# One reordering in three places: the opening of a strided attention and the fronts of two expert stages

## The chip, the cores and the metric

The kernel runs on one core of one Trainium2 chip. The metric is the device time of one execution in microseconds (us). Engines: TensorE (PE; PEld is its weight load), VectorE (DVE), ScalarE (ACT), GpSimd (POOL) and SyncE (SP), which only issues transfers. They run side by side, each in the order of its own program, and wait for one another by semaphores.

## The reference, cut to what matters

Four layers in a row, each with a tanh gate and a residual, over x of 8 batches x 100 tokens x 512:

```python
x = x + tanh(g_xattn[0]) * perceiver_attention(ctx, layernorm(x), mask)
x = x + tanh(g_ffn[0]) * experts_top2_of_4(layernorm(x))      # stage f
x = x + tanh(g_xattn[1]) * strided_attention(layernorm(x), ctx)   # stage g
x = x + tanh(g_ffn[1]) * experts_top2_of_8(layernorm(x))      # stage m
```

The strided attention has 16 heads of 32; head h attends to every 16th context row from row h on, 45 keys per batch and head:

```python
Q = x @ Wq.T + bq;  K = ctx @ Wk.T + bk;  V = ctx @ Wv.T + bv
scores = Q_h @ K_h[h::16].T / sqrt(32)
attn = softmax(scores)
out = concat_h(attn @ V_h[h::16]) @ Wo.T + bo
```

An expert stage takes layernormed tokens, chooses two experts per token by their logits, weighs them with a softmax over the two, and sums `silu(x @ W1) * (x @ W3) @ W2` of both.

## The kernel before, in words

Products in f32 that need more than one pass are made of three products of a high and a low part: ScalarE makes the high part by a copy to the fp32r type, VectorE or GpSimd the low part by subtraction ("split").

**Stage g, `strided_attention`.** TensorE first makes keys and values of four groups of heads (`context(c)`) and the queries of two halves of the batches (`half(h)`) in banks 0 to 3 of PSUM, in turn; ScalarE copies them out (`move_keys`, `move_values`, `move_queries`). The last are `context(3)`, whose keys sit in bank 2 and values in bank 3. Meanwhile ScalarE makes the high parts of the output weights (`high_output_weights`), two of four among the last queries and two after `move_values(3)`, and after them waits for the gate and makes its tanh; VectorE makes the low parts (L2701) and scales the output bias by the gate (L2703, `bo_done`), whereupon GpSimd adds the bias to the residual of 8 batches (L2311).

Then comes the work by batch n. TensorE: `scores(n)` (L2504) in banks 0, 1 or 2, 3 by the parity of n; `element(b)` (L2496), the transposes that turn the values of batch b, in banks 4 to 7, copied by ScalarE (L2393) to `v_nat`; `transposes(n, r)` (L2512) of the probabilities in banks 4 and 5, copied by ScalarE and, as r runs from 0 to 3, `attend(n)` (L2521) in bank 6; `project(n)` (L1265 to L1267 with `g_wo_hi`, `g_wo_lo`) in bank 7. VectorE: `lower(n)`, the row maxima (L2658) and their subtraction (L2661); ScalarE: `exponent(n)` (L2397); VectorE: `divide(n)`, row sums (L2667), reciprocal and multiply (L2669); then `low_output(n)` (L2680), `finish(n)` (L2674).

Before the change TensorE's order at the opening is: wait for all four banks, `scores(0)`, eight elements, `scores(1)`, wait for all element copies, then for n = 0 to 7 `transposes(n, 0..1)`, `scores(n + 2)`, `transposes(n, 2..3)`, `project(n - 1)`, `attend(n)`. VectorE's is low weights, bias, `lower(0)`, `divide(0)`, `lower(1)`, `divide(1)`. ScalarE's is four elements, `exponent(0)`, four elements, `exponent(1)`, then the loop.

**Stages f and m, `gated_experts`.** Both run the same code. Tokens are sorted into slots of 128 by expert, 14 in f and 16 in m. VectorE computes, from rank tables made before, the place of each token in a slot: `picked` (L1880), `filled` (L1884), a chain of some ten linked operations, four comparisons `at_row` (L1909); TensorE sums 16 matmuls (L1752) into the row numbers; VectorE casts them to `rows_at` (L1922), and GpSimd gathers each slot's rows from DRAM by an indirect transfer into `y_acc[:, s]` (L1631). Before the gathers the same `y_acc[:, s]` holds piece s of the raw weights, so gather s waits for the low split of piece s:

```python
if q == 0 and s < DIRECT:
    wait_low(pool, 0, 0, s)
```

The 16 pieces of the first group are split high by ScalarE (L1676) and low by VectorE (L1916). VectorE's order is: maximum and subtraction of the logits (L1876, L1877), `picked`, rank copy (L1881), the chain, three splits, `rows_at` (L1922, L1924, L1925), the fourth split, the gates (L1969 to L1975, eight operations), a wait for the first gather to land, splits 4 to 15 with two tiles of low tokens among them. ScalarE's is four splits, Exp and Tanh and a Silu to load its table, 12 splits, the tokens' high parts (L1686). TensorE transposes slots 0 and 1 (L1765) and goes through the slots (L1780 to L1784), ScalarE and VectorE making silu and product (L1699, L1952).

## Time and profile before

| | us |
|---|---|
| median of 3 runs | 2011.34 |
| lowest and highest | 2009.47 and 2014.04 |
| profiled execution, its time | 2012.05 |
| profiled execution, its span | 2010.3 |
| mean granted TensorE clock | 0.972 of full speed |
| stage f, from its first instruction | from 990.7 |
| stage g, from its first matmul | from 1513.1 |
| stage m, from its first instruction | from 1648.4 |

The span runs from the first to the last instruction of the profiled execution; all times of rows are counted from its start. The clock is the share of 2.4 GHz that the throttle granted. "Busy" leaves out waits and the issuing of transfers.

### The profile page before, as it was taken

The page shows a single profiled execution, that of the slowest core. Times are in us where ns is not written, and L with a number is a line of the kernel's source. Part 1 is how long each engine was busy: PE and PEld are TensorE (multiplying, and loading weights), DVE is VectorE, ACT ScalarE, POOL GpSimd, SP SyncE. Part 2 cuts the span into 40 slices and gives each one's busy share as a digit, 9 for nine tenths or more (in the row PEclk, how much of TensorE's full clock was granted, in tenths as well). Part 3 has the DMA queues.
Part 4 walks back from the last instruction along what each step waited for, and adds up shares of the span by engine and source line. Part 5 has one row for each costly group of instructions (what it writes and reads, how often), then busy time and mean ns, then how long its engine had stood idle before and what let it go on. Part 6 is the DMA issues. An engine that isn't in the chain of part 4 may idle for free. (4 is left out here: it accounts for less than half of the span.)

```text
span 2010.3 us, 35337 instructions
## 1 busy us (share of the span) xinstructions
PE 1888.3 (94%) x12144; PEld 1538.6 (77%) x12144; DVE 1051.9 (52%) x2437; ACT 801.9 (40%) x1733; POOL 648.9 (32%) x529
## 2 busy tenths in 40 slices
PE   7999999999999999999599999999997877999994
PEld 4788787887878787878378888888884766999983
DVE  6526565655656565646553333233345675644564
ACT  4434343433434343433433334233323544555550
POOL 4030202002030302000145553455521215787872
PEclk9999999999999999999799999999998987999997
DMA  7741013121221210010343333133368044635546
GB/s 290 239 137 53 25 41 81 41 81 40 55 66 55 66 47 35 9 27 14 108 120 111 111 115 125 43 114 110 115 231 306 12 160 121 209 138 179 192 153 210
DMA packets 122363, 220.26 MB, mean 110 GB/s; under 512 B 41883, under 2 KB 46779, under 8 KB 120295
## 3 DMA queue, kind: packets, MB, share of 16 engines
q1 hardware_dynamic: 117415, 202.62, 30.3%
q0 software_dynamic: 4800, 15.73, 2.4%
q8 instruction: 85, 1.39, 0.3%
q14 instruction: 63, 0.52, 0.1%
HBM read 189.47 MB, written 28.03 MB: 108 GB/s over the span
## 5 line engine op out<-in xcount | busy, mean ns | idle before, releaser
L588 POOL TENSOR_TENSOR a_cols<-a_cols,a_moments_b 128x722 f32<-128x722 f32 x32 | 58.4, 1825 | 546.0 <-DMA a_moments_b<-a_moments_dram 518.0
L757 PE MATMUL a_kv_ps<-a_kvin_hi,a_wk_hi 128*128 128x512 f32 (+1 forms) x512 | 196.0, 383 | 0.0
L758 PE MATMUL a_kv_ps<-a_kvin_lo,a_wk_hi 128*128 128x512 f32 (+1 forms) x512 | 179.9, 351 | 0.0
L759 PE MATMUL a_kv_ps<-a_kvin_hi,a_wk_lo 128*128 128x512 f32 (+1 forms) x512 | 179.8, 351 | 0.0
L1952 DVE TENSOR_TENSOR f_h_sb<-f_h_sb,f_banks 128x256 f32<-128x256 f32 x112 | 47.2, 421 | 242.3 <-ACT f_h_sb L1699 241.8
L669 ACT ACTIVATE a_probs<-a_probs,a_neg_max 100x822 f32<-100x822 f32 x128 | 125.9, 984 | 101.3 <-DVE a_neg_max L1056 101.3
L1265 PE MATMUL f_banks<-f_wab_hi,f_x_hi 128*128 x392 | 161.2, 411 | 0.0
L1699 ACT ACTIVATE f_h_sb<-f_banks 128x256 f32<-128x256 f32 x112 | 43.0, 384 | 291.9 <-PE f_banks L1267 263.9
L757 PE MATMUL a_kv_ps<-a_wv_hi,a_kvin_hi 128*128 128x512 f32 (+1 forms) x384 | 156.7, 408 | 0.3 <-DVE a_k_lo L1049 0.3
L1267 PE MATMUL f_banks<-f_wab_hi,f_x_lo 128*128 x392 | 154.2, 393 | 0.0
L1266 PE MATMUL f_banks<-f_wab_lo,f_x_hi 128*128 x392 | 153.0, 390 | 0.0
L759 PE MATMUL a_kv_ps<-a_wv_hi,a_kvin_lo 128*128 128x512 f32 (+1 forms) x384 | 152.2, 396 | 0.0
L758 PE MATMUL a_kv_ps<-a_wv_lo,a_kvin_hi 128*128 128x512 f32 (+1 forms) x384 | 151.4, 394 | 0.0
L659 ACT ACTIVATE a_probs_t<-a_t_ps 128x400 f32<-128x400 f32 x128 | 64.3, 502 | 187.4 <-PE a_t_ps L843 187.4
L652 ACT ACTIVATE a_k_hi<-a_kv_ps 128x512 fp32r<-128x512 f32 (+1 forms) x128 | 65.8, 514 | 175.8 <-PE a_kv_ps L759 167.2
L1265 PE MATMUL m_banks<-m_wab_hi,m_x_hi 128*128 x448 | 133.7, 298 | 0.0
L1623 POOL TENSOR_TENSOR f_wy_lo<-f_raw,f_wy_hi 128x512 fp32r<-128x512 f32 x60 | 77.3, 1288 | 160.1 <-ACT f_wy_hi L1676 160.1
L1056 DVE CUSTOM_DVE_ANT_0 a_probs<-a_s_ps,a_mask_add 100x822 f32<-100x822 f32 x128 | 128.5, 1004 | 0.0
L1267 PE MATMUL m_banks<-m_wab_hi,m_x_lo 128*128 x448 | 126.7, 283 | 0.0
L1266 PE MATMUL m_banks<-m_wab_lo,m_x_hi 128*128 x448 | 126.3, 282 | 0.0
L1069 DVE COPY a_probs_t<-a_t_ps 128x300 f32<-128x300 f32 x128 | 59.8, 467 | 124.3 <-PE a_t_ps L843 124.0
L843 PE MATMUL a_t_ps<-a_ident,a_probs 100*128 100x100 f32 x896 | 122.6, 253 | 0.7 <-DVE a_probs_t L1069 0.7
(440 smaller groups left out, 4901.8 us busy)
## 6 DMA issues: line engine op xcount, KB each, us to landing
f_raw<-f_pieces SPq DMA_DIRECT2D x94, 256.0 KB, 2.6
m_raw<-m_pieces SPq DMA_DIRECT2D x92, 256.0 KB, 2.9
f_wab_raw<-f_pieces SPq DMA_DIRECT2D x42, 512.0 KB, 5.9
m_wab_raw<-m_pieces SPq DMA_DIRECT2D x42, 512.0 KB, 6.2
a_rows<-ctx_rows SPq DMA_DIRECT2D x8, 1536.0 KB
a_cols<-ctx_cols SPq DMA_DIRECT2D x8, 1444.0 KB
ahead_piece<-g_ctx SPq DMA_DIRECT2D x2, 2880.0 KB
a_moments_b<-a_moments_dram SPq DMA_DIRECT2D x7, 722.0 KB
```

The costliest lines, as they stand in the source:

```text
L652: nc.scalar.activation(k_hi[:, c:c + w], kv_bank("k", n, part)[:, 0:w], ACT.Copy).then_inc(k_hi_done, 1)
L659: nc.scalar.activation(probs_t[:, x, M * a:M * b], t_ps[:, 0:M * (b - a)], ACT.Copy).then_inc(ta_done, 1)
L669: nc.scalar.activation(probs[0:M, x, 0:KEYS], probs[0:M, x, 0:KEYS], ACT.Exp, scale=-1.0, bias=neg_max[0:M, x:x + 1], accum_out=row_sum[0: ...
L757: nc.tensor.matmul(out, hi_l, hi_r, start=first, stop=False)
L758: nc.tensor.matmul(out, hi_l, lo_r, start=False, stop=False)
L759: return nc.tensor.matmul(out, lo_l, hi_r, start=False, stop=last)
L843: ins = nc.tensor.transpose(t_ps[:, M * (t - a):M * (t - a) + M], probs[0:M, x, KFROM[t]:KFROM[t] + P], ident[0:M, 0:M])
L1056: nc.vector.tensor_tensor_reduce(out=probs[0:M, x, 0:KEYS], in0=s_ps[0:M, x, 0:KEYS], in1=mask_add[0:M, :], scale=-1.0, scalar=3.0e38, op0 ...
L1265: nc.tensor.matmul(out, left_hi, right_hi, start=start, stop=False)
L1266: nc.tensor.matmul(out, left_hi, right_lo, start=False, stop=False)
L1267: return nc.tensor.matmul(out, left_lo, right_hi, start=False, stop=stop)
L1623: nc.gpsimd.tensor_tensor(split_dst(wab_lo, wy_lo, c), raw_of(q, n), split_dst(wab_hi, wy_hi, c).bitcast(F32), ALU.subtract).then_inc(wlo_ ...
```

## The change

In stage g: ScalarE makes the gate's tanh behind the first query copy of the second half, and all four high output weights ahead of `move_keys(3)`. The two small transfers of gate and bias go ahead of that of the output weights on SP's queue. VectorE scales the bias before the low output weights, and does `lower(0)`, `lower(1)`, `divide(0)`, `divide(1)`. TensorE does `scores(0)` when banks 0 to 2 are free, `scores(1)` when bank 3 is, then eight elements in banks 4 to 7 and 0 to 3. ScalarE copies two elements between the first exponentials, four after them, two after the first batch's probabilities.

In f and m: VectorE moves the logits' maximum, subtraction and rank copy behind `at_row`; two splits instead of three stand before `rows_at`, the other two behind the gates. VectorE waits after `rows_at[:, 0]` for GpSimd to have issued the first gather. ScalarE does 12 splits before Exp and 4 after.

```diff
@@ gated_experts, GpSimd: gather_rows
+                    if n == 0:
+                        pool.sem_inc(gather_begun, 1)
@@ ScalarE
-            for c in range(AHEAD):
+            for c in range(3 * AHEAD):
                 split(0, 0, c)
             act.wait_ge(shift_done, 1)
...
-            for c in range(AHEAD, LAST):
+            for c in range(3 * AHEAD, LAST):
@@ VectorE
-            own.link(nc.vector.tensor_reduce(l_max[0:M, :], logits[0:M, :, :], axis=AX.X, op=ALU.max))
-            nc.vector.tensor_tensor(p_exp[0:M, :, :], ...).then_inc(shift_done, 1)
-
             for k in range(TOP):
-                nc.vector.tensor_scalar(picked[0:M, :, k, :], ...)
-            own.link(nc.vector.tensor_copy(rank[0:M, :, :], tables.rank[0:M, :, :]))
+                ins = nc.vector.tensor_scalar(picked[0:M, :, k, :], ...)
+            own.link(ins)
             dve.wait_ge(count_ready, 2)
...
-            for c in range(AHEAD - 1):
+            own.link(nc.vector.tensor_reduce(l_max[0:M, :], logits[0:M, :, :], axis=AX.X, op=ALU.max))
+            nc.vector.tensor_tensor(p_exp[0:M, :, :], ...).then_inc(shift_done, 1)
+            own.link(nc.vector.tensor_copy(rank[0:M, :, :], tables.rank[0:M, :, :]))
+            for c in range(AHEAD - 2):
                 split(0, 0, c)
             dve.wait_ge(rows_ready, 1)
             nc.vector.tensor_copy(rows_at[:, 0, :], banks[:, CONST, 0:SLOTS]).then_inc(rows_done, 1)
+            dve.wait_ge(gather_begun, 1)
...
-            split(0, 0, AHEAD - 1)
...
             dve.sem_inc(gates_done, 1)
+            for c in range(AHEAD - 2, AHEAD):
+                split(0, 0, c)
             dve.wait_ge(rows_loaded[0], 16)
@@ strided_attention
-        S, VN, TP, O, Y = 0, 4, 4, 6, 7
+        S, TP, O, Y = 0, 4, 6, 7
+        VN = (4, 5, 6, 7, 0, 1, 2, 3)
@@ SP
             sp.wait_ge(mid_done, B)
-            sp.dma_start(wo_raw[:, :, :], wo_t).then_inc(wo_loaded, 16)
             sp.dma_start(tanh_g[:, :], ...).then_inc(c_loaded, 16)
             sp.dma_start(bo_b[0:M, :], ...).then_inc(c_loaded, 16)
+            sp.dma_start(wo_raw[:, :, :], wo_t).then_inc(wo_loaded, 16)
@@ ScalarE
             for n in range(KD, 2 * KD):
                 move_queries(n)
+                if n == KD:
+                    act.wait_ge(c_loaded, 32)
+                    nc.scalar.activation(tanh_g[:, :], tanh_g[:, :], ACT.Tanh).then_inc(tanh_done, 1)
                 if n >= KD + 2:
                     high_output_weights(n - KD - 2)
+            for k in range(2, KD):
+                high_output_weights(k)
             move_keys(3)
             move_values(3)
-            for k in range(2, KD):
-                high_output_weights(k)
-            act.wait_ge(c_loaded, 32)
-            nc.scalar.activation(tanh_g[:, :], tanh_g[:, :], ACT.Tanh).then_inc(tanh_done, 1)
...
-            for b in range(HB):
+            exponent(0)
+            element(0)
+            element(1)
+            exponent(1)
+            for b in range(2, 6):
                 element(b)
-            exponent(0)
-            for b in range(HB, B):
-                element(b)
-            exponent(1)
             for n in range(B):
                 for r in range(4):
                     move_t(n, r)
+                if n == 0:
+                    element(6)
+                    element(7)
@@ TensorE
             def element(b):
                 if b >= 4:
-                    pe.wait_ge(vn_done, b - 3)
+                    pe.wait_ge(sub_done, b // 2 - 1)
...
             def scores(n):
+                if n in (2, 3):
+                    pe.wait_ge(vn_done, 2 * n + 2)
...
-            for n in range(4):
+            for n in range(3):
                 pe.wait_ge(bank_free[n], BANK_USES)
             scores(0)
+            pe.wait_ge(bank_free[3], BANK_USES)
+            scores(1)
             for b in range(B):
                 element(b)
-            scores(1)
-            pe.wait_ge(vn_done, B)
             for n in range(B):
                 pe.wait_ge(p_done, n + 1)
+                if n == 0:
+                    pe.wait_ge(vn_done, 1)
                 transposes(n, 0)
+                if n == 0:
+                    pe.wait_ge(vn_done, 2)
                 transposes(n, 1)
@@ VectorE
+            dve.wait_ge(tanh_done, 1)
+            nc.vector.tensor_scalar(bo_b[0:M, :], ...).then_inc(bo_done, 1)
             for k in range(KD):
                 dve.wait_ge(wo_hi_done, k + 1)
                 nc.vector.tensor_tensor(wo_lo[:, k, :], ...).then_inc(wo_lo_done, 1)
-            dve.wait_ge(tanh_done, 1)
-            nc.vector.tensor_scalar(bo_b[0:M, :], ...).then_inc(bo_done, 1)
-            for n in range(2):
-                lower(n)
-                divide(n)
+            lower(0)
+            lower(1)
+            divide(0)
+            divide(1)
```

The first `attend` and the first `project` also wait for the third and fourth element copy, whose banks they take.

## Rows read from the trace of the kernel before

**Rows 1.** The page: busy time and share of each engine.
```profile
PE 1888.3 (94%) x12144; PEld 1538.6 (77%) x12144; DVE 1051.9 (52%) x2437; ACT 801.9 (40%) x1733; POOL 648.9 (32%) x529
```

**Rows 2.** Timeline, steady attention: start, us, engine, line, operation, count [idle before].
```profile
1605.31 0.89 PE L2512 MATMUL g_banks<-ahead_rest_w,ahead_piece 100*45 100x100 f32 x8
...
1611.62 0.89 PE L2512 MATMUL g_banks<-ahead_rest_w,ahead_piece 100*45 100x100 f32 x8
```

**Rows 3.** Timeline of TensorE, the attention's opening.
```profile
1569.27 1.13 PE L2504 MATMUL g_banks<-g_k_bd,ahead_rest_x 128*100 128x180 f32 x6 [0.77 <-ACT g_v_t L2333]
...
1570.54 3.74 PE L2496 MATMUL g_banks<-ahead_rest_w,g_v_t 128*45 128x128 f32 x32
1574.12 1.08 PE L2504 MATMUL g_banks<-g_k_bd,ahead_rest_x 128*100 128x180 f32 x6
...
1578.14 0.85 PE L2512 MATMUL g_banks<-ahead_rest_w,ahead_piece 100*45 100x100 f32 x8 [2.64 <-DVE ahead_piece L2669]
...
1588.86 0.48 PE L1265 MATMUL g_banks<-g_wo_hi,ahead_xn_hi 128*100 128x512 f32 x1 [0.95 <-DVE ahead_xn_lo L2680]
```

**Rows 4.** Timeline of VectorE, the same stretch.
```profile
1572.10 0.90 DVE L2658 TENSOR_REDUCE ahead_rest_w<-g_banks 100x16 f32<-100x720 f32 x1
...
1576.04 1.95 DVE L2669 TENSOR_TENSOR ahead_piece<-ahead_piece,ahead_rest_w 100x720 f32<-100x720 f32 x1
...
1586.19 0.90 DVE L2667 TENSOR_REDUCE ahead_rest_w<-ahead_piece 100x16 f32<-100x720 f32 x1 [0.87 <-ACT ahead_piece L2397]
...
1587.42 0.91 DVE L2669 TENSOR_TENSOR ahead_piece<-ahead_piece,ahead_rest_w 100x720 f32<-100x720 f32 x1
1588.24 0.56 DVE L2680 TENSOR_TENSOR ahead_xn_lo<-g_banks,ahead_xn_hi 128x400 fp32r<-128x400 f32 x1
```

**Rows 5.** Timeline of ScalarE, the same stretch.
```profile
1566.14 2.27 ACT L2324 ACTIVATE g_k_bd<-g_banks,ahead_rest_w 32x360 f32<-32x360 f32 x4 [1.48 <-PE g_banks L2452]
...
1570.17 1.28 ACT L2387 ACT_TABLE_LOAD   x1
...
1571.58 2.01 ACT L2393 ACTIVATE sums_y_got<-g_banks 45x512 f32<-45x512 f32 x4
...
1579.79 0.80 ACT L2397 ACTIVATE ahead_piece<-ahead_piece 100x720 f32<-100x720 f32 x1 [3.08 <-DVE ahead_piece L2661]
```

**Rows 6.** Timeline of GpSimd, the same stretch.
```profile
1572.28 10.52 POOL L2311 TENSOR_TENSOR ahead_x_mid<-ahead_x_mid,g_bo_b 100x512 f32<-100x512 f32 x8 [53.82 <-DVE g_bo_b L2703]
```

**Rows 7.** Windows: length, busy (count) of PE, PEld, DVE, ACT, POOL; PEclk, DMA.
```profile
1584.00:1586.00 2.00, 2.00 (x12) 1.97 (x11) 1.29 (x2) 0.64 (x1) 0.00 (x0) 0.50 0.00 0
```

**Rows 8.** Timeline, front of the f stage, ScalarE and VectorE.
```profile
990.70 2.19 ACT L1676 ACTIVATE f_wab_hi<-f_sums_ahead 128x512 fp32r<-128x512 f32 x4 [5.02 <-PEq L2774]
...
991.55 0.19 DVE L1876 TENSOR_REDUCE f_l_max<-logits 100x8 f32<-100x32 f32 x1 [2.74 <-PEq L2774]
...
992.26 0.19 DVE L1884 TENSOR_TENSOR f_scratch<-f_banks,f_tables 128x28 f32<-128x28 f32 x1
...
1001.04 0.68 DVE L1916 TENSOR_TENSOR f_wab_lo<-f_sums_ahead,f_wab_hi 128x512 fp32r<-128x512 f32 x1
...
1003.23 0.17 DVE L1975 TENSOR_TENSOR gates<-gates,f_p_sum 100x16 f32<-100x16 f32 x1
```

**Rows 9.** Timeline of GpSimd, first and last gather of f (14) and m (16).
```profile
1001.13 1.66 POOL L1631 DMA_INDIRECT f_sums_ahead<-f_xn,f_rows_at  x1 [5.38 <-DVE f_rows_at L1922]
...
1018.67 0.95 POOL L1631 DMA_INDIRECT f_sums_ahead<-f_xn,f_rows_at  x1 [0.30 <-issue]
...
1659.69 1.59 POOL L1631 DMA_INDIRECT m_sums_ahead<-m_xn,m_rows_at  x1 [3.49 <-DVE m_rows_at L1922]
...
1679.78 0.95 POOL L1631 DMA_INDIRECT m_sums_ahead<-m_xn,m_rows_at  x1 [0.30 <-issue]
```

**Rows 10.** Timeline of ScalarE, end of its stall in f and in m.
```profile
1021.63 0.38 ACT L1699 ACTIVATE f_h_sb<-f_banks 128x256 f32<-128x256 f32 x1 [3.74 <-PE f_banks L1784]
...
1683.07 0.28 ACT L1699 ACTIVATE m_h_sb<-m_banks 128x128 f32<-128x128 f32 x1 [9.38 <-remote]
```

More of the change, by code:

```diff
@@ L1423, in gated_experts @@
         start_ready = sem("start_ready")
+        gather_begun = sem("gather_begun")
         x_done = sem("x_done")
@@ L2392, in element @@
                     act.wait_ge(mid_done, B)
-                nc.scalar.activation(v_nat[0:J, b, :], banks[0:J, VN + b % 4, :], ACT.Copy).then_inc(vn_done, 1)
+                nc.scalar.activation(v_nat[0:J, b, :], banks[0:J, VN[b], :], ACT.Copy).then_inc(vn_done, 1)
             def exponent(n):
@@ L2493, in element @@
                 if b >= 4:
-                    pe.wait_ge(vn_done, b - 3)
+                    pe.wait_ge(sub_done, b // 2 - 1)
                 for c in range(KD):
-                    ins = nc.tensor.transpose(banks[0:J, VN + b % 4, P * c:P * c + P], v_t[:, c, J * b:J * b + J], ident[:, :])
+                    ins = nc.tensor.transpose(banks[0:J, VN[b], P * c:P * c + P], v_t[:, c, J * b:J * b + J], ident[:, :])
                 ins.then_inc(vn_ready, 1)
@@ L2518, in attend @@
                     pe.wait_ge(olo_done, n)
+                else:
+                    pe.wait_ge(vn_done, O - TP + 1)
                 for h in range(H):
```

7 lines of the change are left out of this document (4 added, 3 removed).

## The prediction

> **What bounds the kernel now.** The page comes first: TensorE is busy 94% of the span [rows 1], so a change pays only where TensorE stands still. Then the timeline by engine, over three stretches that the diff touches: the opening of the strided attention and the fronts of the two expert stages (f and m).
>
> In the attention's steady part TensorE is the limit: the transposes of one batch start 6.31 us after those of the batch before [rows 2], with no idle time in front of them. Whatever the opening saves is therefore kept until the stage's end, once the opening is over. The opening is not so. Its first score matmul waits 0.77 us for the copy of the last values, then come scores(0), 32 element transposes, scores(1), and then 2.64 us of idle time before the first transposes of probabilities, at 1578.14. The first product with the output weights, project(0), starts only at 1588.86, after 0.95 us of waiting for VectorE [rows 3]. VectorE is the chain: its first reduction starts at 1572.10 although TensorE had left scores(0) for the elements at 1570.54, because low output weights and the bias stand in front; the division's multiply takes 1.95 us where the later one takes 0.91; and maxima(1) stand behind division(0) [rows 3, 4]. ScalarE adds a table load of 1.28 us and eight element copies, four of them ahead of the first exponential [rows 5]. GpSimd adds the bias from 1572.28 to 1582.80, beside the slow multiply [rows 6]. The granted clock was 0.50 from 1584 to 1586, that is 1.2 GHz, after that idle time [rows 7].
>
> **The attention's opening, part by part.** I lay out the new order with the durations shown.
>
> *Gate, bias, low weights.* The Tanh table load and the Tanh (1.48 us) move behind the first query copy of the second half, where ScalarE waits for TensorE, and the gate is back about when the next copy is due: nothing. VectorE is idle there too. The bias additions then run from some 1560 to 1570.5, and they meet the four low-weight subtractions instead of the division. If each of these took the 1.95 us of the slow multiply, the last would end near 1570, about when scores(0) is ready; so I cost it at nothing, at worst 0.5 us. Without this cover they would cost what they cost now. The two small transfers moved before the 1 MB of output weights on SP's queue wait behind the same context pieces and have over 10 us of slack, as have the weights: nothing.
>
> *Scores first.* scores(0) no longer waits for the values' copy but for the keys' copy, which ends at 1568.41 [rows 5]: start near 1568.6 instead of 1569.27, end 1570.0. scores(1) follows at once, to 1571.4 (1.27 us from start to start, 1570.54 less 1569.27, [rows 3], and some 0.15 for the last results). Elements 0 to 3 follow to 1573.3 (3.74 / 8 = 0.47 each), 4 and 5 need maxima(0) to be subtracted, 6 and 7 need maxima(1): the last ends near 1575.2.
>
> *VectorE.* Maximum 0.90 and subtraction 0.91 for batch 0 give 1571.9, for batch 1 1573.8. The first exponential (0.80, [rows 5]) ends at 1572.7 and is no longer waited for. A division is 2.14 us (from 1586.19 to 1588.33, [rows 4]): it ends at 1575.95. So the first transposes start near 1576.1 instead of 1578.14: 2.0 us. Of these 1.04 is the multiply without its neighbour on GpSimd.
>
> *ScalarE.* Exponential 0, two elements, exponential 1, four elements (2.01 for four, [rows 5]) end at 1576.65, just when scores(2) wants banks 0 and 1 free (1577.0). This new wait is the tightest; if it is late, all waits. Four copies of probabilities end at 1579.75, elements 6 and 7 at 1580.75, exponential 2 at 1581.55.
>
> *The end of the opening.* Division 1 ends at 1578.1 (behind division 0) and is not waited for any more. Division 2 ends at 1583.7, the low output (0.56) at 1584.3; TensorE has finished the transposes of batch 1 at 1584.0 if it keeps 2.4 GHz. project(0) starts at 1584.4 instead of 1588.86: **4.5 us**. From there TensorE is full and the gain stays. Bounds: 2.0 from the first transposes alone, 4.9 if only TensorE counts. If the clock falls as in [rows 7], the 3.1 us of batch 1's transposes and scores (0.85 + 1.4 + 0.85) take up to 6.2; half of them at 1.2 GHz costs 1.6, less 0.4 of slack: a gain of 3.3, and 1.8 with all of them.
>
> **The fronts, part by part.** Maximum, subtraction and rank copy leave the chain that makes the row numbers: VectorE's `filled` starts 0.42 us earlier (of the 0.71 between 991.55 and 992.26 the two comparisons keep an estimated 0.29, [rows 8]). They now stand beside TensorE's placement matmuls in place of one split; two splits go behind the gates. The first gather then starts 0.42 earlier. ScalarE makes 12 high splits first (0.55 each from 990.70, [rows 8]: to 997.3), waits for the subtraction at some 998.8, and loads Exp after it (1.28, and some 0.25): the exponential is there by 1000.4, and VectorE wants it at 1002.2, so I cost that at nothing.
>
> The first gather takes 1.66 us in f and 1.59 in m, the last ones 0.95 [rows 9]. A split runs on VectorE from 1001.04 to 1001.72, over the gather's start [rows 8]; its rest of 0.59 is about the 0.71 too much. The new wait `gather_begun` keeps VectorE still until GpSimd has issued it, so I take 0.95. First rows thus land 1.1 us earlier in each stage.
>
> The Trainium skill's page "SBUF — State Buffer", section "Who interferes with whom", speaks against that: a VectorE operation with two SBUF inputs contends with a GpSimd operation that reads SBUF, and it infers that descriptor generation needs the write side. By the page the gather stays at 1.66 and the rows land only 0.42 earlier.
>
> What it costs: behind the wait stand two small operations (0.4), eight for the gates (1.7, to 1003.40 in [rows 8]), and then splits 2 and 3. Raw weights lie where gathers 2 and 3 write, so GpSimd waits for these splits. Gather 0 from 1000.7 to 1001.65, small ones and gates to 1004.0, split 2 to 1004.7: gather 2 starts near 1004.9, where it stood at 1004.34 (1001.13 + 1.66 + 0.95 and twice the 0.30 between two, [rows 9]). It then meets split 3 (up to 0.4). The train of gathers ends about 0.7 us **later** in each stage, though TensorE does not need row tile 2 until far later.
>
> Which of the two counts hangs on ScalarE. In m it sits 9.38 us until 1683.07, in f 3.74 until 1021.63, though its input was ready [rows 10] (the row of f names TensorE's L1784 as releaser, but the tile that this instruction reads was complete before the stall); both ends lie 3.0 to 3.3 us after the last gather's start (1018.67, 1679.78, [rows 9]), about when that gather lands. If it comes back with the end of the train, the fronts lose 2 x 0.7 = 1.4. If its stalls keep their lengths, they gain 2 x 1.1 = 2.2. Ends -2.2 and +1.4; I take 0, with the early rows worth something and the late train costing something.
>
> The page "Runtime: NRT & Kernel Launch", section "Instruction fetch mechanics", says that engines fetch instructions by a DMA queue of their own; a fetch that queues beside the gathers would be such a stall. No row here names it.
>
> **The sum.** -4.5 + 0 = -4.5 us. The profiled execution took 2012.05 us, 1.75 more than its span; it becomes 2007.5. It lies 0.7 above the median of 2011.34, for which I predict **2006.8**.
>
> **The rivals.**
> 1. *ScalarE follows the gather train* (18%): -4.5 + 1.4 = -3.1, 2008.2. For it: both ends in [rows 10]. Where the first gather keeps its 1.66, each train is 0.7 later still: -1.7, 2009.6; that makes up 5 of the 18. The page on SBUF named above has this last form.
> 2. *The fronts keep their whole gain* (15%): -4.5 - 2.2 = -6.7, 2004.6. For it: TensorE starts on its first tile 1.1 earlier; against it: the long stall in m.
> 3. *TensorE's clock still falls in the opening* (12%): gain 3.3 to 1.8, 2008.0 to 2009.5. For it: pauses of 0.9, 0.8 and 0.4 remain; against it: they are a third of the old ones.
> 4. *The other side* (8%): the stall on ScalarE has no fixed length; f has 3.74 where m has 9.38 at the same place. ScalarE now ends its splits some 2 us later in the front, and if this puts f in the state of m, it costs 5.6: +1.1, 2012.5. It decides from 4.5 us of added stall on; beyond 8.5, with m lengthened as well, the kernel is over 0.2% slower. About half of this case.
> 5. *The opening does little* (5%): scores(2) waits for the six element copies and the elements among the exponentials cost what they save: 0 to -1.5, 2010 to 2011.
>
> **How the numbers follow.** The forecast has 42%, with its own range of 2005.4 to 2008.2 (opening 3.1 to 4.9, fronts +-1). The range for 8 in 10 takes in rivals 1 to 3: 2003.8 to 2009.8. Measurement of this kernel can tell about 0.2%, 4.0 us, from no change. Faster than that is below 2007.3: two thirds of the forecast, rival 2 and a piece of rivals 1 and 3 (the opening at 4.9), 0.28 + 0.15 + 0.06 = 0.49. Slower: half of rival 4 and 0.02 for a wait that I have not seen, 0.06. The rest, 0.45, is within 0.2%.
>
> **What would show it.** The first transposes of probabilities (matmul, L2512 of before) 2.0 us earlier against the last values' matmul, project(0) 4.5 earlier, its division's multiply at 0.91, bias additions ended before 1571, granted clock 1.00 throughout, then a period of 6.3. In the fronts: first gather 0.95 long and 0.42 earlier, gather 2 later than before, and the stalls of ScalarE against the last gather. Wrong would be: a long idle time before scores(2), a half clock in the opening, a stall in f above 8 us, or a table loaded twice among the queries.

## The result and the profile after

| | before | after |
|---|---|---|
| median, us | 2012.11 (4 runs) | 1996.58 (4 runs) |
| lowest and highest, us | 2009.47, 2014.04 | 1995.12, 2000.27 |
| profiled execution, its span, us | 2010.3 | 1993.1 |
| mean granted TensorE clock of it | 0.972 | 0.975 |

The ratio is 0.9928, 95% interval 0.9916 to 0.9939: 14.5 us faster by the ratio (15.5 between the medians), where 4.5 were forecast and 2006.8 us. The time lies below the whole range. The page of the changed kernel shows TensorE 6 us less busy than in [rows 1], with the same 12144 matmuls, so part of it comes from the clock:

```profile
PE 1881.9 (94%) x12144; PEld 1535.4 (77%) x12144; DVE 1051.5 (53%) x2437; ACT 801.8 (40%) x1733; POOL 652.4 (33%) x529
```

I cut both spans at the same five instructions. To ScalarE's first split in f it is 2.1 us shorter (990.70 to 988.58), a stretch in which no code was changed; from there to the last values' matmul of the attention's opening 6.5 (576.40 to 569.91); from there to project(0) 5.3 (21.76 to 16.50); to the first split in m 0.3 (59.59 to 59.31); from there to the end 3.05 (361.85 to 358.80). The sum is the 17.2 between the spans. Of the 6.5, 4.7 lie in f's front; the other 1.8 lie in the 500 us behind it, which take 503.4 to 506.0 us in the fourteen profiles of this document, whatever the kernel (505.4 before, 503.6 here, but 506.0 in `e2_fronts`). The opening is near the forecast. The surprise is in the stretches that begin with the fronts of f and m.

**The opening.** Timeline of TensorE, then of VectorE, of the changed kernel (start, us, engine, line, operation, count, idle before):

```profile
1558.49 1.39 PE L2462 MATMUL g_banks<-sums_piece_end,ahead_wv 128*32 128x360 f32 x16
1559.95 1.13 PE L2516 MATMUL g_banks<-g_k_bd,ahead_rest_x 128*100 128x180 f32 x6
...
1562.44 3.71 PE L2506 MATMUL g_banks<-ahead_rest_w,g_v_t 128*45 128x128 f32 x32
1567.12 0.89 PE L2524 MATMUL g_banks<-ahead_rest_w,ahead_piece 100*45 100x100 f32 x8 [0.97 <-DVE ahead_piece L2688]
...
1574.99 0.48 PE L1265 MATMUL g_banks<-g_wo_hi,ahead_xn_hi 128*100 128x512 f32 x1 [0.69 <-DVE ahead_xn_lo L2699]
```

```profile
1553.91 1.55 DVE L2722 TENSOR_TENSOR g_wo_lo<-g_wo_raw,g_wo_hi 128x512 fp32r<-128x512 f32 x1 [2.87 <-ACT g_wo_hi L2382]
1556.09 4.47 DVE L2722 TENSOR_TENSOR g_wo_lo<-g_wo_raw,g_wo_hi 128x512 fp32r<-128x512 f32 x3 [0.62 <-ACT g_wo_hi L2382]
1561.42 0.91 DVE L2677 TENSOR_REDUCE ahead_rest_w<-g_banks 100x16 f32<-100x720 f32 x1 [0.86 <-PE g_banks L2516]
...
1566.16 0.91 DVE L2688 TENSOR_TENSOR ahead_piece<-ahead_piece,ahead_rest_w 100x720 f32<-100x720 f32 x1
```

Read against the start of the last values' matmul (1567.10 before, 1558.49 here), the first transposes come 8.63 us after it instead of 11.04, so 2.4 earlier (forecast 2.0), and project(0) 16.50 instead of 21.76 (forecast 4.5 less). The idle time before the first transposes fell from 2.64 [rows 3] to 0.97, the multiply from 1.95 [rows 4] to 0.91. VectorE now waits 0.86 us for scores(0) instead of being late for them. The low weights did meet the bias additions, which start at 1551.13 and take 11.77 us; they lengthened from 0.69 and 1.29 for two to 1.55 and 4.47 for three, yet ended 0.86 before they would have cost anything. The clock in the windows stayed at 1.00, where [rows 7] had 0.50 (columns as there). A half clock between the first transposes and the end of project(0) is in all six profiles with the old order of scores and elements, and in none of the eight with the new:

```profile
1569.00:1571.00 2.00, 1.37 (x27) 1.13 (x29) 1.67 (x3) 1.25 (x3) 0.00 (x0) 1.00 0.00 0
1571.00:1573.00 2.00, 2.00 (x42) 1.85 (x33) 0.94 (x2) 2.00 (x6) 0.00 (x0) 1.00 0.00 0
```

**The fronts.** Timeline of GpSimd in f, the changed kernel's gathers:

```profile
998.61 1.20 POOL L1632 DMA_INDIRECT f_sums_ahead<-f_xn,f_rows_at  x1 [5.38 <-DVE f_rows_at L1925]
1000.11 0.95 POOL L1632 DMA_INDIRECT f_sums_ahead<-f_xn,f_rows_at  x1 [0.31 <-issue]
1001.63 1.15 POOL L1632 DMA_INDIRECT f_sums_ahead<-f_xn,f_rows_at  x1 [0.57 <-DVE f_wab_lo L1916]
...
1007.57 3.91 POOL L1632 DMA_INDIRECT f_sums_ahead<-f_xn,f_rows_at  x1 [0.30 <-issue]
...
1019.29 0.95 POOL L1632 DMA_INDIRECT f_sums_ahead<-f_xn,f_rows_at  x1 [0.30 <-issue]
```

Counted from ScalarE's first split (990.70 and 988.58), the first gather starts at 10.03 instead of 10.43 us, as forecast, and takes 1.20 instead of 1.66 [rows 9]. The first transposes of tokens, which wait for its rows, come 0.83 us earlier (1002.26 and 1005.21), and in m 0.94. The last gather starts at 30.7 instead of 28.0, because of one gather of 3.91 us; in m it starts at 30.9 instead of 31.3. And ScalarE (its timeline in f, then in m; L1702 is the silu of a tile):

```profile
1012.29 0.39 ACT L1702 ACTIVATE f_h_sb<-f_banks 128x256 f32<-128x256 f32 x1 [2.16 <-PE f_banks L1787]
...
1015.69 0.39 ACT L1702 ACTIVATE f_h_sb<-f_banks 128x256 f32<-128x256 f32 x1 [1.58 <-issue]
...
1021.76 0.38 ACT L1702 ACTIVATE f_h_sb<-f_banks 128x256 f32<-128x256 f32 x1 [4.24 <-remote]
```

```profile
1657.95 0.62 ACT L1679 ACTIVATE m_wy_hi<-m_raw 128x512 fp32r<-128x512 f32 x1
1668.30 0.28 ACT L1702 ACTIVATE m_h_sb<-m_banks 128x128 f32<-128x128 f32 x1 [9.72 <-remote]
```

Both stalls still end 2.5 and 3.1 us after the start of the last gather, and they are as long as ever (3.74 and 9.38 in [rows 10]). But they stand elsewhere. I count tiles from 0. Before, ScalarE was stuck ahead of the silu of tile 1 in both stages. Now it is stuck ahead of tile 3 in f and of tile 2 in m: two tiles and one tile more are done before it stops. In f the 3.74 us of [rows 10] were also only the last of three holds. Two more stand ahead of it in the kernel before, one of them ahead of tile 0, and the changed kernel has neither:

```profile
1013.73 0.39 ACT L1699 ACTIVATE f_h_sb<-f_banks 128x256 f32<-128x256 f32 x1 [5.09 <-remote]
1017.30 0.60 ACT L1686 ACTIVATE f_x_hi<-f_banks 128x512 fp32r<-128x512 f32 x1 [3.19 <-remote]
```

("remote": the trace names no releaser on this core.) A useful measure of a whole front is the time from ScalarE's first split to its first split of the next group of hidden units. It was 71.01 in f and 64.02 in m and is 66.35 and 60.90: 4.7 and 3.1 us less.

### The profile page after: what moved, and what is told of

Same layout as the page of the kernel before. It is cut to its first block and busy times, and to the rows that moved or that the text cites. A ratio compares the mean times of both kernels' runs of the same rounds, so it can differ in the third digit from the quotient of the medians.

```text
span 1993.1 us, 35343 instructions
## 1 busy us (share of the span) xinstructions
PE 1881.9 (94%) x12144; PEld 1535.4 (77%) x12144; DVE 1051.5 (53%) x2437; ACT 801.8 (40%) x1733; POOL 652.4 (33%) x529
## 3 DMA queue, kind: packets, MB, share of 16 engines
q1 hardware_dynamic: 117415, 202.62, 30.9%
## 5 line engine op out<-in xcount | busy, mean ns | idle before, releaser
L1702 ACT ACTIVATE f_h_sb<-f_banks 128x256 f32<-128x256 f32 x112 | 43.1, 385 | 289.1 <-PE f_banks L1267 261.9
L659 ACT ACTIVATE a_probs_t<-a_t_ps 128x400 f32<-128x400 f32 x128 | 64.3, 502 | 187.4 <-PE a_t_ps L843 187.4
```

Source lines behind the costliest of these rows:

```text
L659: nc.scalar.activation(probs_t[:, x, M * a:M * b], t_ps[:, 0:M * (b - a)], ACT.Copy).then_inc(ta_done, 1)
```

## The experiments

All kernels compute the whole reference. Each time below is a median with its ratio to the kernel before. Single executions of one kernel spread by up to 15 us, most of it along with the mean granted clock (before: 2005.3 us at 0.974, 2019.9 at 0.967). So I also fitted one slope for the clock and one level for each kernel to the 176 timed executions whose clock is on record (75 of them of the kernel before): 1.45 us for 0.001 of clock, standard deviation 1.7 us around it. "At 0.972" is a kernel's level in that fit; each +- is a 95% interval. Before is at 2011.0 +- 0.4, after at 2000.0 +- 1.7: of the 14.5 us some 11 are the change at equal clock. The other 3 to 4 go with the mean clock of 0.974 in its four runs against 0.971 before. A level at equal clock credits a kernel with nothing for a clock that it has raised itself, and part of this rise seems to be of that kind. The mean granted clock over m's front is 0.74 to 0.77 in the seven profiles with the last stall at tile 1, 0.76 to 0.80 in the four with it at a later tile, and 0.82 in the two kernels below that have no stall and no other long wait there. The other part comes and goes, and is told in the last section.

**1. Each half alone.** `e1_opening` is the kernel before with the edits in `strided_attention`, `e2_fronts` the kernel before with the edits in `gated_experts`; the diffs are the two parts of the change shown above.

> The kernel before with the strided attention's part of the change alone; both expert fronts as before. Theory A (the opening's gain is local, 5.3 us by the two traces, from the last V matmul to the first project): 2012.1 - 5.3 = 2006.8 us, the f and m stages as long as in the trace of before (522.2 and 361.9 us from ScalarE's first split), the g stage about 130. Rival B (the longer-standing clock and the earlier end of g also shorten m, and the fronts' edits do nothing there): m falls by 3 as well, 2003.8. Rival C (the g stage's 5.9 us hang on how f ended): under 2 us gained, 2010 or more.

> The kernel before with the edits of the two expert fronts alone; the strided attention as before. Theory A (the fronts keep what they gain: f 6.2 and m 3.05 us by the two traces, because ScalarE gets one or two tiles further before its long stall): 2012.1 - 9.3 = 2002.8 us; ScalarE's long stall stands at Silu(3) in f and at Silu(2) in m. Rival B (most of the 9.3 us are another state of TensorE's clock, brought by the opening): 2 us or less gained, 2010 or more. Forecast of the prediction (fronts give nothing): 2012.

Opening alone: 2005.24, 0.9972 (0.9959 to 0.9984), at 0.972 2005.5 +- 1.0. Fronts alone: 2006.15, 0.9971 (0.9957 to 0.9986), at 0.972 2005.0 +- 1.0. So 5.5 and 6.0 us at equal clock, and together 11: the parts add within the fit. By the ratios they are 5.6 and 5.8, some 3 us short of the 14.5 of both. From the last values' matmul to project(0), the opening takes 16.50 us in the profile of `e1_opening` as in that of the changed kernel, and 21.76 in `e2_fronts` as before. The front takes 66.35 in f and 59.44 in m in `e2_fronts`, 72.48 and 63.33 in `e1_opening`. A front does not repeat as well as the opening: five profiles with VectorE's old order have 71.0 to 72.7 in f and 63.3 to 64.3 in m, four with the new order 66.4 to 67.0 and 59.4 to 61.3. The gain is thus 4 to 6.3 us in f and 2 to 4.8 in m, by the pair of profiles that one takes. Theory A of both stands in its places. But it put the fronts at 9.3 us, since it took over what the clock had added to two profiles.

**2. The opening's halves.** In `e7_weights` only gate, bias and output weights move:

```diff
 for n in range(KD, 2 * KD):
     move_queries(n)
+    if n == KD:
+        act.wait_ge(c_loaded, 32)
+        nc.scalar.activation(tanh_g, ...Tanh)
     if n >= KD + 2:
         high_output_weights(n - KD - 2)
+for k in range(2, KD):
+    high_output_weights(k)
 move_keys(3)
 move_values(3)
-for k in range(2, KD): high_output_weights(k)      # and the tanh
```

In `e8_scores` only the order of scores, elements, maxima and divisions changes, with the element banks:

```diff
 scores(0)
+scores(1)
 for b in range(B): element(b)        # now in banks 4 to 7, 0 to 3
-scores(1)
...
-lower(0); divide(0); lower(1); divide(1)
+lower(0); lower(1); divide(0); divide(1)
```

> The kernel before with one half of the opening's edits: gate and bias loaded ahead of the output weights, the gate's tanh and the high output weights among the queries, the bias's multiply ahead of the low weights. Scores, elements and maxima in the old order. The opening alone gave 0.28%, some 6 us. Theory A (this half takes the table load and ScalarE's four weight copies out of the last stretch, 1.28 + 2.01 us, of which the first exponential stood behind a part): 1 to 3 us gained, 2009 to 2011 us. Rival B (the old order of scores and elements hides it): under 1 us, 2011 to 2012. Rival C: it carries nearly all, 2006.

> The kernel before with the other half of the opening's edits: both scores first, the elements through eight banks, both subtractions ahead of the first division, elements and exponentials interleaved on ScalarE; gate, bias and output weights in the old order. Theory A (this half carries the larger part, but the first exponential still stands behind the weights' copies and the table load): 3 to 5 us gained, 2007 to 2009 us. Rival B (the halves need each other: the exponential is released by neither alone): under 1.5 us, over 2010 us. Rival C: it carries all of 6 us, 2006.

Measured: 2011.26, 0.9992 (0.9983 to 1.0002), and 2011.44, 0.9998 (0.9988 to 1.0009); at 0.972 2009.9 and 2010.4, each +- 1.1. Neither alone can be told from no change, though the profile shows each at work. From the last values' matmul to project(0):

```profile
1584.05 0.47 PE L1265 MATMUL g_banks<-g_wo_hi,ahead_xn_hi 128*100 128x512 f32 x1 [0.95 <-DVE ahead_xn_lo L2681]
```

```profile
1584.23 0.48 PE L1265 MATMUL g_banks<-g_wo_hi,ahead_xn_hi 128*100 128x512 f32 x1 [0.95 <-DVE ahead_xn_lo L2693]
```

The first row is of `e7_weights`, the second of `e8_scores`. The last values' matmuls start at 1565.02 and 1564.91, so 19.03 and 19.32 us, against 21.76 and 16.50. The halves save 2.7 and 2.4 in place, and both together 5.3: in place they add, and neither needs the other. By the times, 2011.26 and 2011.44, rival B of both holds; by the places, `e7_weights` has what its theory A says, and `e8_scores` somewhat less. The clock-fitted times show 1.1 and 0.6, each +-1.2. In `e7_weights` seven of the twelve matmuls of project(0) take 0.63 us each instead of 0.40, at half clock, and from project(0) to m it needs 60.69 instead of 59.5: about 1.2 given back right there, which leaves 1.5 and agrees with the fit. `e8_scores` gives nothing back there (59.55). Both profiles have VectorE's long wait late in m (last section), 3 to 4 us; whether their other executions had it too is not known, so where the gain of `e8_scores` went stays open.

**3. Within the fronts.** `e3_no_begun` takes out the new wait and its count from the changed kernel. `e4_exp_early` puts ScalarE's old order back, `for c in range(AHEAD)` ahead of the exponential. `e6_act_order` is the kernel before with ScalarE's new order alone. `e10_logits` is the kernel before with that order and, on VectorE, only the logits' operations and the rank copy moved:

```diff
-own.link(tensor_reduce(l_max, logits))
-tensor_tensor(p_exp, logits, l_max, subtract).then_inc(shift_done)
 ...                                        # row numbers
+own.link(tensor_reduce(l_max, logits)); tensor_tensor(p_exp, ...)
 for c in range(AHEAD - 1): split(0, 0, c)
```

> The changed kernel without VectorE's wait for the first gather: the pair numbers' two operations run as soon as the rows' numbers are cast, beside the first gather. Theory A (this wait only shortens the first gather's issue, 1.20 and 1.09 against 1.66 and 1.59 us, and the train of gathers shifts by half a microsecond): 1996.6 + 0 to 1 = 1996.6 to 1997.6 us. Rival B (the wait is what lets ScalarE run on before the stall): the stalls go back to Silu(1), and 5 us or more of the fronts' 9.3 are lost, 2001.6 or more.

> The changed kernel with ScalarE's splits in the old order: four, then the exponential and its table loads, then the rest. The shifted logits now come late, so ScalarE stands after four splits until VectorE has made them, some 5.5 us, and the last splits and TensorE's first tokens come later. Theory A (where ScalarE's long stall stands depends on when it runs, not on how many instructions came before): the stall ends at the same time against the gathers, but fewer tiles are done before it: 1 to 5 us lost over two fronts, 1998 to 2002 us. Rival B (the long stall's place goes by the order of instructions on ScalarE: the one change in ScalarE's order moved it): it goes back to Silu(1) in both stages and all of the 9.3 us are lost, 2006. Rival C: the order is hidden, under 1 us.

> The kernel before with ScalarE's order in the fronts alone: twelve splits ahead of the exponential instead of four, nothing on VectorE moved. With the changed kernel the old order on ScalarE cost some 3 to 4 us. Theory A (the fronts' gain of 5.8 us needs both: the order on ScalarE alone brings the last splits no earlier, since the exponential never waited in the kernel before): within 2 us of the kernel before, 2010 to 2012 us. Rival B (the order on ScalarE alone moves the long stall to a later tile): 2006 to 2008 us.

> The kernel before with ScalarE's new order in the fronts and, on VectorE, only the logits' maximum, the shift and the copy of the ranks moved behind the row numbers; the splits stand where they stood, the pair numbers' operations wait for nothing. Theory A (the fronts' gain comes from what VectorE does between the row numbers and the sixteenth low weight, that is from the two splits and the one wait as well): the first gather 0.4 us earlier, but only 0 to 3 us gained of the 5.8 that both fronts gave, 2009 to 2012 us. Rival B (the earlier row numbers alone carry it): 2006 us, ScalarE's stall in f at Silu(3).

| kernel | median, us | ratio, 95% | at 0.972 | front f | front m |
|---|---|---|---|---|---|
| `e3_no_begun` | 1999.21 | 0.9932 (0.9911 to 0.9953) | 2000.3 +- 1.4 | 66.46 | 60.30 |
| `e4_exp_early` | 2001.66 | 0.9950 (0.9933 to 0.9967) | 2002.7 +- 1.2 | 67.14 | 62.85 |
| `e6_act_order` | 2012.24 | 1.0003 (0.9990 to 1.0015) | 2011.6 +- 1.1 | 72.65 | 64.28 |
| `e10_logits` | 2011.24 | 0.9990 (0.9981 to 1.0000) | 2009.4 +- 1.1 | 67.55 | 64.44 |

The wait for the first gather does nothing: without it the gather takes 1.20 and 1.12 us, and the time is the same. What had lengthened it was the 0.68 us split beside it [rows 8]; in `e10_logits`, where that split still stands there, the gather takes 1.66 and 1.59 again. That is no general rule: before, the sixth gather of f (1008.17 to 1009.12) takes 0.95 although VectorE makes two splits beside it, from 1008.17 to 1009.50. ScalarE's order alone does nothing either, and with the other edits it is worth 2.7 (+-2.1) at equal clock: in m the stall goes back to tile 1, in f it comes at tile 2. The logits' move alone shortens f's front by 3.5, and m's not at all; m needs the splits behind the gates as well. Theory A of `e10_logits` holds, and the simpler idea that each edit has a price of its own does not. In m the place of the stall goes with the start of the silu of tile 0. In the seven profiles without pacing where that is 20.4 to 23.1 us after ScalarE's first split (before, `e1`, `e4`, `e6`, `e7`, `e8`, `e10`) the last stall stands at tile 1; in the four where it is 19.0 to 19.4 (after, `e2`, `e3`, `e11`) it stands at tile 2 or later. In f this start alone does not tell: with 20.78 and 21.19 us (`e10`, `e4`) ScalarE gets to tile 2, with 20.79 (`e8`) only to tile 1. And the four fronts of f in which it gets to tile 3 (after, `e2`, `e3`, `e11`) are the four whose seventh gather takes 3.9 us. That pause in the train, which is no edit, may have let the third tile through; without it, `e10` and `e4` have fronts of 67.55 and 67.14, against 66.35. So that the stall's place sets the length is shown; what sets the place is shown in part. `e4_exp_early` bears out its theory A: same end, one tile fewer, within the 1 to 5 us.

**4. The code's place.** `e11_shift` puts 32 instructions on ScalarE ahead of the tokens:

```diff
+for _ in range(32):
+    act.sem_inc(shifted, 1)
 act.wait_ge(expert_done, 2)
```

> The changed kernel with 32 more instructions on ScalarE in each front, each only a count on a semaphore that nobody waits for, placed where ScalarE idles 2.7 to 2.9 us before its first tokens. It moves the code behind them by 32 instructions. Theory A (ScalarE's long stall stands at a place of the code, where it needs its next instructions while the gathers run): the stall begins some three to four tiles earlier, at Silu(0) or ahead of it, ends as before 2.4 to 3.3 us after the last gather, and the kernel takes 2 to 8 us more, 1999 to 2005 us. Rival B (its place hangs on time or on the gathers alone): stall at Silu(3) and Silu(2) as in the changed kernel, 1996 to 1998 us.

1996.04, 0.9916 (0.9900 to 0.9933). In m ScalarE stalls ahead of tile 2 for 9.19 us, where it did without the 32 instructions; in f it is held twice, 2.24 us after the silu of tile 2 and 1.57 us later on, until 2.6 us after the last gather's start. My theory A fell, rival B holds: 32 instructions more do not bring the stall three tiles forward.

**5. The train of gathers.** In all 22 fronts of the eleven kernels without pacing, the last stall ended 2.4 to 3.3 us after the last gather's start. So `e5_paced` gives the changed kernel's gathers a pace:

```diff
 if q == 0 and s < DIRECT:
     wait_low(pool, 0, 0, s)
+if q == 0 and s >= 6:
+    pool.wait_ge(st_ready[0], s - 3)     # tile s - 4 turned
 nc.gpsimd.indirect_dma_start(y_acc[:, s, :], ...)
```

> The changed kernel with one wait added on GpSimd in both fronts: from the seventh gather on, each waits until TensorE has turned the token tile four places ahead of it, so that the gathers come as they are needed instead of back to back. In the six profiles so far ScalarE's last long stall ended 2.4 to 3.3 us after the last gather of the train was issued, in all twelve fronts. Theory A (the train itself keeps ScalarE standing, and any pause in it lets it run): no stall over 3 us, 3 to 10 us gained on the changed kernel, 1987 to 1994 us. Rival B (ScalarE is let go only when the whole train is out): the train now waits for TensorE, which waits for ScalarE, so the stalls lengthen or stay, and GpSimd's low weights come later: 1997 to 2005 us. Rival C (the stalls go, but the later low weights hold the projections or the ring of raw weights by as much): within 1 us of 1996.6.

2003.38, 0.9957 (0.9942 to 0.9972): slower than the change. Every stall for which the trace has no releaser was gone, and another wait had come. ScalarE in f, then in m:

```profile
1041.42 0.63 ACT L1681 ACTIVATE f_wy_hi<-f_raw 128x512 fp32r<-128x512 f32 x1 [8.15 <-DMA f_raw<-f_pieces]
```

```profile
1688.75 0.63 ACT L1681 ACTIVATE m_wy_hi<-m_raw 128x512 fp32r<-128x512 f32 x1 [6.80 <-DMA m_raw<-m_pieces]
```

The waits of SP's queue over f's front (who waited for whom, us, times, longest) say why:

```profile
SPq L1531 <- POOL f_wy_lo L1624: 39.4, 8, 25.6
```

The raw output weights go through a ring of four buffers, and GpSimd, which frees them by its low parts, had these queued behind all of its gathers. So theory A was right about the stalls. Rival C named the mechanism of the price and put it too low: it expected the time of the change, and the kernel lost 2.6 us to it at equal clock and 6.8 between the medians. `e9_paced_low` puts the low parts among the gathers:

```diff
 nc.gpsimd.indirect_dma_start(...)
+if q == 0 and s >= 7:
+    upto = LAST + (PIECES - LAST) * min(s - 6, SIZE[0] - 3) // (SIZE[0] - 3)
+    low_weights(0, lowered, upto); lowered = upto
```

> The paced gathers again, and with them GpSimd's first low output weights among the gathers instead of behind them all: after each gather from the eighth on, the low parts of the pieces that ScalarE has split by then. In the paced run the long stalls were gone, but ScalarE waited 8.15 us in f and 6.80 us in m for a raw weight whose place in the ring of four was held by low weights queued behind the gathers. Theory A (both waits go): f some 4 us and m some 2 us shorter than in the changed kernel, 1988 to 1993 us. Rival B (GpSimd's order now holds the gathers back, each low weight 1.28 us): 1996 to 2001 us.

**1989.65 us**, 0.9883 (0.9866 to 0.9899), at 0.972 1994.6 +- 1.8, theory A: the fastest kernel here, 23.5 us below the one before and some 7 below the change (1989.65 against 1996.58; 5.4 at equal clock, from four executions each). ScalarE and GpSimd in m's front; tiles follow each other every 2 us, and low weights stand between gathers:

```profile
1662.14 0.28 ACT L1709 ACTIVATE m_h_sb<-m_banks 128x128 f32<-128x128 f32 x1 [0.95 <-PE m_banks L1794]
...
1664.12 0.28 ACT L1709 ACTIVATE m_h_sb<-m_banks 128x128 f32<-128x128 f32 x1 [0.77 <-issue]
...
1666.09 0.28 ACT L1709 ACTIVATE m_h_sb<-m_banks 128x128 f32<-128x128 f32 x1 [0.26 <-PE m_banks L1794]
```

```profile
1663.30 0.94 POOL L1636 DMA_INDIRECT m_sums_ahead<-m_xn,m_rows_at  x1 [1.45 <-PE m_banks L1775]
1664.27 1.29 POOL L1624 TENSOR_TENSOR m_wy_lo<-m_raw,m_wy_hi 128x512 fp32r<-128x512 f32 x1
1665.72 0.96 POOL L1636 DMA_INDIRECT m_sums_ahead<-m_xn,m_rows_at  x1 [0.16 <-issue]
```

The front of m takes 51.69 us instead of 60.90. That of f takes 66.46, as with the change, though its stall of 4.24 is gone. TensorE needs 3.4 us for a tile there (from silu to silu, 1012.29 and 1015.69 above), and ScalarE catches up after the stall: the silu of tile 5 starts 37.42 us after the first split with the stall and 37.52 without. A stall at tile 3 in f is nearly free. One at tile 1 is not: there tile 5 comes at 42.00 before, and at 38.07 in the next kernel, which is the one before without the stall.

`e12_paced_before` has both pacing edits on the kernel before, with nothing of the change:

> The kernel before with the paced gathers and the low output weights among them, and nothing of the change. From ScalarE's first split to the first split of the second group of hidden units, a front took 71.0 us in f and 64.0 in m before, 66.4 and 60.9 after the change, 66.5 and 51.7 with the change and the pacing. Theory A (the long stalls behind the train of gathers set the fronts, and the change gained by moving work ahead of them): pacing alone brings both fronts to within 2 us of the change with pacing, f 68 and m 53 or less, and the change's own gain there shrinks to under 1.5 us in each; the kernel takes 1998 to 2003 us. Rival B (the front edits gain by themselves, by 2 us at the first tokens, stalls or no stalls): f stays at 70 or more, 2004 us or more.

1995.88, 0.9911 (0.9890 to 0.9933), at 0.972 1997.5 +- 1.5: theory A, and 2 us better than it said. The fronts take 67.01 and 52.56 us. Once the gathers are paced, the edits of the change save 0.55 in f (67.01 less 66.46) and 0.87 in m (52.56 less 51.69), no more than the first rows come earlier (0.83 and 0.94); without the pace they save 4.7 and 3.1. Here is the first split of the second group in m, before, after, and in this kernel (start less 1648.45, 1634.30 and 1643.34 gives the front):

```profile
1712.47 2.18 ACT L1676 ACTIVATE m_wab_hi<-m_raw 128x512 fp32r<-128x512 f32 x4
```

```profile
1695.20 2.19 ACT L1679 ACTIVATE m_wab_hi<-m_raw 128x512 fp32r<-128x512 f32 x4
```

```profile
1695.90 2.19 ACT L1683 ACTIVATE m_wab_hi<-m_raw 128x512 fp32r<-128x512 f32 x4
```

## Why the prediction was wrong

**Opening, -4.5: right in mechanism, a little small.** The first transposes came 2.4 us earlier (2.0 forecast), project(0) 5.3 (4.5 forecast, and above the upper bound of 4.9), and alone the opening gives 5.5 at equal clock. The multiply is 0.91 long, the clock stayed at 1.00, the table is loaded once, the copies of exponentials and elements came in the order laid out. The low weights cost nothing, under the cover of the wait for the values. The term missed 0.8 us in two even parts: from the last values' matmul to the first transposes it laid out 9.0 us and 8.63 were taken, and from there to project(0) 8.3 and 7.87 were.

**Fronts, 0: the step that failed.** I wrote "Ends -2.2 and +1.4; I take 0". Measured: -6.0 alone at equal clock. Both ends rested on one picture: the stall either keeps its length, or comes back with the end of the train. The second half of it was right, in every unpaced front; in f the stall even ended 2.2 us later than before, and the front was 4.7 us shorter. What I did not ask is where the stall *begins*. It ends with the train, so it costs what could have been done meanwhile, and that depends on how many tiles are through before it. Rows that came 0.8 and 0.9 us earlier (1.1 forecast) brought tile 0's silu 2.5 and 2.7 us earlier, since less of the holds stood ahead of it, and one or two more tiles were through, each worth up to 3.4 us in f and 2 in m. In m that leaves 1 of the 3.1 us; the clock that stood at its lower level for less of the front is the likely rest, but no run holds it fixed. And the 3.74 us that the prediction took for f's stall left out the 5.09 and 3.19 ahead of it. `e12_paced_before` shows it from the other side: take the stall away, and the front edits are worth 0.55 and 0.87 us.

**The first gather.** 0.42 earlier was right (0.40). I took 0.95 for its length; it is 1.20 and 1.09. The page "SBUF — State Buffer" of the Trainium skill, section "Who interferes with whom", infers that a VectorE operation of this kind does not hold up the descriptors of a GpSimd transfer, and so spoke for an unchanged 1.66. The traces do not bear this out for the first gather, which is long beside the split (1.66 and 1.59 in `e10_logits`) and shorter without it; a later gather that took 0.95 beside two splits agrees with it. The wait itself, which I credited with this, is not needed.

**The late train.** Forecast 0.7 later; gather 2 came 0.6 earlier in f against the stage's start (13.05 against 13.65), and the train ended 2.7 later in f and 0.4 earlier in m. The late end in f did not lengthen its front.

**The rest.** 3 to 4 us go with a higher mean clock, for which the prediction had no term. The clock over m's front (0.74 before, 0.79 after, 0.82 without a stall) and the mean clock of `e11_shift`, 0.974 in four more runs, speak for the change as the cause of part of it; how much is not shown.

**The rivals.** Rival 2 had the right sign, but priced the fronts at 2.2, because it too held the stalls fixed in length. Rival 1's mechanism, that ScalarE follows the train, is the true one for the stall's end; its price had the wrong sign. Rival 4 said that the stall has no fixed length and can grow by 5.6 for the price of some 2 us of delay. That is the same lever seen from its other end, and `e4_exp_early` shows it: stall at tile 1 in m, 10.75 us. Rivals 3 and 5 fell: the clock stayed at 1.00 in the opening, and nothing waited ahead of scores(2).

**What stays open.** What ScalarE lacks in the stalls. Its input is there, the trace names no releaser, and 32 more instructions did not move it in m. The page "Runtime: NRT & Kernel Launch" of the Trainium skill, section "Instruction fetch mechanics", has engines fetch instructions by DMA; no run here shows that a fetch was what ended a stall. Shown is only that it hangs on the back-to-back train: with pauses in it there is no stall of this kind in any of the six paced fronts.

## What to carry to other kernels

When a stall ends with an outside event, don't price it by its length or its end: ask which work is through before it begins, for that can multiply a head start: rows 0.8 and 0.9 us earlier made the fronts 4.7 and 3.1 us shorter. Pace a train of indirect gathers by their consumer instead of issuing all at once, but look first what is queued behind them on the issuing engine: here the ring of raw weights took back all of the gain and 2.6 us more until its release was moved among the gathers. And where executions differ by 15 us with the granted clock, compare lengths between two fixed instructions before believing a median. The opening repeated here to 0.02 us (16.49 to 16.51 in the seven kernels that have all of its edits, 21.76 to 21.77 in four of the five that have none). But the fifth, `e12_paced_before`, took 22.56, with a longer spell of half clock, and a front repeats only to 1 or 2 us.

## What the hardware showed unexpectedly

Time hangs on the clock of a few short stretches, in parts of the kernel that were the same in all of them. Windows of the kernel before around 70 us (columns as in [rows 7]): TensorE idles for 1.5 us, and then the granted clock is at its lower level, 1.2 GHz, for a while.

```profile
68.00:70.00 2.00, 0.55 (x4) 0.29 (x3) 2.00 (x4) 1.41 (x3) 0.00 (x0) 1.00 1.06 374
70.00:72.00 2.00, 1.48 (x11) 1.34 (x12) 2.00 (x3) 1.98 (x2) 0.00 (x0) 0.75 1.06 371
72.00:74.00 2.00, 2.00 (x9) 1.35 (x7) 1.97 (x3) 0.41 (x2) 0.00 (x0) 0.50 1.10 430
```

The changed kernel's profile does not have it. The window from 60 to 80 us, before and after:

```profile
60.00:80.00 20.00, 18.02 (x82) 13.86 (x81) 16.46 (x32) 10.27 (x17) 0.00 (x0) 0.91 1.07 372
```

```profile
60.00:80.00 20.00, 18.03 (x89) 14.18 (x88) 17.16 (x36) 11.79 (x19) 0.00 (x0) 1.00 1.07 373
```

Of fourteen profiles, four have no such fall ahead of f, and f begins at 988.6 to 989.0; nine have one (eight here, one between 950 and 975), and f begins at 989.8 to 990.8; one has both, and f begins at 992.9. One fall costs 1 to 2 us, and the same kind of idle time sometimes brings it and sometimes not. I have no rule for it from these runs. The 2.1 us that the change seemed to gain ahead of f are this.

Late in m something larger comes and goes. There VectorE makes low output weights while GpSimd makes low weights too, both by subtractions with two inputs in SBUF. In eight profiles they share. Timeline of VectorE, changed kernel:

```profile
1924.44 2.87 DVE L1916 TENSOR_TENSOR m_wy_lo<-m_raw,m_wy_hi 128x512 fp32r<-128x512 f32 x2 [0.23 <-ACT m_wy_hi L1679]
...
1927.63 3.05 DVE L1916 TENSOR_TENSOR m_wy_lo<-m_raw,m_wy_hi 128x512 fp32r<-128x512 f32 x2
```

In the other six (`e1`, `e3`, `e4`, `e7`, `e8`, `e9`) VectorE gets hardly anything until GpSimd is through. VectorE, GpSimd and TensorE of `e3_no_begun`, and three windows of it:

```profile
1926.76 9.16 DVE L1914 TENSOR_TENSOR m_wy_lo<-m_raw,m_wy_hi 128x512 fp32r<-128x512 f32 x2 [0.23 <-ACT m_wy_hi L1677]
```

```profile
1921.08 13.70 POOL L1624 TENSOR_TENSOR m_wab_lo<-m_wab_raw,m_wab_hi 128x512 fp32r<-128x512 f32 x11
```

```profile
1936.18 0.47 PE L1792 MATMUL m_banks<-m_ident,m_h_sb 128*128 128x128 f32 x1 [7.30 <-DVE m_h_sb L1952]
```

```profile
1930.00:1932.00 2.00, 0.00 (x0) 0.00 (x0) 2.00 (x1) 0.00 (x0) 2.00 (x2) 1.00 0.00 0
1932.00:1934.00 2.00, 0.00 (x0) 0.00 (x0) 2.00 (x1) 0.00 (x0) 2.00 (x3) 0.70 0.00 0
1934.00:1936.00 2.00, 0.00 (x0) 0.00 (x0) 2.00 (x3) 0.00 (x0) 0.78 (x1) 0.50 0.00 0
```

Two subtractions take 9.16 us instead of 2.87, TensorE waits 7.30 us for the product behind them, and its granted clock falls to 0.50 within that wait. The mean clock from 1915 to 1955 is 0.91 in these six profiles and 1.00 in the eight others. With the old fronts, m takes 361.85, 362.42 and 363.35 us where they share (before, `e6`, `e10`) and 365.3 to 365.7 where VectorE starves (`e1`, `e7`, `e8`); with the new ones 358.80, 357.74 and 359.69 (after, `e2`, `e11`) against 362.72 (`e3`). Less its front, m takes 297.9 to 298.9 us in the eight profiles that share, 301.6 to 302.5 in five of the others, and 304.5 in `e9`, where some 2 us of it lie behind the last matmul. So this is 3 to 4 us of an execution, and the low mean clock is its mark as much as its cause. The code is the same in all fourteen; what tips it was not found. Keeping GpSimd and VectorE apart there was not tried.

Two more. One gather took 3.3 to 3.9 us instead of 0.95 in seven of the 28 trains, always the seventh of its train, and only in kernels with all of the front edits; what makes it long was not found. In the two profiles of m where it came without pacing (`e2_fronts`, `e3_no_begun`), ScalarE got to tile 4 before its last stall, instead of tile 2: a pause of 3 us in the train seems enough to let it run on. And GpSimd's bias additions (L2317) slow VectorE's subtractions in the opening from 0.65 to 1.5 us each.
